# One eviction, one place to turn back and one pair of normalising instructions for the self and cross outputs of a step in a decoder kernel

## What is computed

```python
x = x + self_attention(layernorm(x), Wv, bv, Wo, bo)      # 16 heads of 8
x = x + cross_attention(layernorm(x), ctx, ctx)           # 16 heads of 8, no projection
x = x + experts(layernorm(x), router_w, routing_bias, sw1, sw2, sw3, ew1, ew2, ew3)
# attention: softmax(q k^T / sqrt(8)) v for each head
```

## Times and profile before

| | |
|---|---|
| median of the timed runs | 447.25 us (446.73 to 450.13, 3 runs) |
| span of the profiled execution | 447.9 us |
| PE busy | 420.6 us (94%), 5570 instructions |
| DVE busy | 312.5 us (70%), 767 instructions |
| ACT busy | 300.6 us (67%), 685 instructions |
| POOL busy | 300.5 us (67%), 517 instructions |
| attention steps | from about 10 to about 265 us |
| granted TensorE clock, mean | 0.985 |

### The profile page before, as it was taken

How to read it: one execution, slowest core, us unless ns; L and a number is a source line. 1 busy time by engine, 2 the same in 40 slices (tenths; PEclk the granted TensorE clock), 3 DMA queues, 4 the chain that set the end, 5 groups by cost and what they waited for, 6 DMA issues and landing times. The chain is left out here.

```text
span 447.9 us, 16458 instructions
## 1 busy us (share of the span) xinstructions
PE 420.6 (94%) x5570; PEld 314.2 (70%) x5571; DVE 312.5 (70%) x767; ACT 300.6 (67%) x685; POOL 300.5 (67%) x517
## 2 busy tenths in 40 slices
PE   7889999999999999999999999999999999999990
PEld 4545655555665655555565567899998899999990
DVE  5568999989999999999999854773333444545540
ACT  7858888788888888788888865432222465666650
POOL 8547768677877868687787655278888754444442
PEclk9999999999999999999999999899999999999995
DMA  6243444444444444453433379812222355530010
GB/s 108 37 83 46 77 52 56 69 53 80 57 80 65 70 74 60 88 64 63 46 57 39 32 131 198 268 44 71 77 80 76 85 129 137 137 105 25 27 35 0
DMA packets 181088, 34.51 MB, mean 77 GB/s; under 512 B 147347, under 2 KB 178582, under 8 KB 181024
## 3 DMA queue, kind: packets, MB, share of 16 engines
q1 hardware_dynamic: 170944, 23.63, 33.2%
q0 software_dynamic: 2864, 6.36, 4.1%
q10 hardware_dynamic: 7216, 3.69, 2.9%
HBM read 20.13 MB, written 15.74 MB: 80 GB/s over the span
## 5 line engine op out<-in xcount | busy, mean ns | idle before, releaser
L1162 DVE TENSOR_TENSOR gT<-gT,psum 128x384 f32<-128x384 f32 x66 | 36.6, 554 | 74.2 <-PE psum L744 51.8
L975 ACT ACTIVATE gT<-psum 128x384 f32<-128x384 f32 x70 | 34.1, 487 | 49.4 <-PE psum L744 36.0
L504 POOL DMA_INDIRECT out<-yrow,token x38 | 37.0, 973 | 40.7 <-DVE yrow L1281 26.5
L443 POOL TENSOR_TENSOR k_s<-pT,hmask_sb 128x1024 f32<-128x1024 f32 x32 | 60.9, 1903 | 2.1 <-ACT pT L904 2.0
L758 PE MATMUL psum<-wdn_sb,gT 128*128 (+1 forms) x420 | 59.9, 279 | 2.0 <-DVE yrow L1281 1.0
L409 POOL TENSOR_SCALAR xn_s<-rows_all,mv 128x128 f32<-128x128 f32 x32 | 19.4, 607 | 56.6 <-DVE mv L1060 37.7
L744 PE MATMUL psum<-fhT,wtile 128*128 128x128 f32 x456 | 57.2, 275 | 0.0
L758 PEld LDWEIGHTS psum<-wdn_sb,gT 128*128 128x128 f32 x420 | 52.4, 192 | 5.0 <-issue 3.9
L744 PEld LDWEIGHTS psum<-fhT,wtile 128*128 128x128 f32 x456 | 53.9, 192 | 0.1
L744 PE MATMUL psum<-hT_all,wup_sb 128*128 (+1 forms) x384 | 49.2, 280 | 0.0
L849 ACT COPY prT_x<-psum 128x512 f32<-128x512 f32 x64 | 34.6, 589 | 20.7 <-PE psum L554 20.4
(11 more groups left out here) (150 smaller groups left out, 890.0 us busy)
## 6 DMA issues: line engine op xcount, KB each, us to landing
ring<-sorted_rows SPq DMA_DIRECT2D x30, 130.0 KB
sorted_rows<-nowhere_row SPq DMA_DIRECT2D x38, 65.0 KB, 2.3
wup_sb<-in_wup SPq DMA_DIRECT2D x7, 352.0 KB, 9.6
attention_out<-on_s SPq DMA_DIRECT2D x64, 32.0 KB, 2.9
ring<-in_ctxv SPq DMA_DIRECT2D x64, 32.0 KB, 3.3
orow<-attention_out SPq DMA_DIRECT2D x32, 64.0 KB
sorted_rows<-nowhere_row SPq DMA_DIRECT2D x3, 650.0 KB, 9.1
cross_keys<-in_ctxk ACTq DMA_DIRECT2D x14, 128.0 KB, 3.1
```

Of the source, the lines that this page charges most:

```text
L443: nc.gpsimd.tensor_tensor(k_s[:], pT[:].rearrange("p (b k) -> p b k", b=NB).unsqueeze(2).broadcast_to([P, NB, HG, S]), hmask_sb[:, 0:HG].u ...
L504: pool.indirect_dma_start(out=out, out_offset=bass.IndirectOffsetOnAxis(ap=token[p][:, 0:1], axis=0), in_=yrow[p][:, :], in_offset=None, b ...
L975: nc.scalar.activation(gT[p][:].rearrange("p c q -> p (c q)"), ps_gate[p][:, 0:CH * P], ACT.Silu).then_inc(sem("f_act"), 1)
L1162: nc.vector.tensor_tensor(g, g, ps_up[p][:, 0:CH * P], ALU.mult).then_inc(sem("f_g"), 1)
```

## The change

`oT`, `rden` and `on` become one tile each with a kind index, and so do the two banks' slices (`ps_wT`, `weighed`). `kinds(t)` is the slice of kinds that are weighed in step t: only self for t = 2 to 4, both for t = 5 to 33, only cross for t = 34 to 36. ACT makes one copy of what is live, after both weighings. PE turns back both at the place of the self output, with one semaphore for the two. DVE inverts and normalises both at the place of the self output, the start of the next step. SP (for the write of the self output) and POOL (for the add of the cross output) now wait for the one `on` semaphore. In the hand-written tail of PE the turning back of the cross outputs moves as well: that of unit 29 stands after `turn_rows(2)`, that of unit 30 before `keep_clock(2, bank[4])`, that of unit 31 where it was.

```diff
+        WEIGHED = {"s": LAG["soft_s"], "x": LAG["pv_x"]}
+        def turned_back(t):
+            return t - LAG["soft_s"] + 1
+        def kinds(t):
+            live = [KIND[k] for k in "sx" if 0 <= t - WEIGHED[k] < U]
+            return slice(live[0], live[-1] + 1)
...
-            def turn_back(k, u):
-                pe.wait_ge(sem(f"{k}_oe"), at(u))
-                for g in range(G):
-                    last = nc.tensor.transpose(ps_w[k][:, P * g:P * (g + 1)], oT[k][:, g, :], id_sb[:])
-                last.then_inc(sem(f"{k}_ot"), 1)
+            def turn_back(t):
+                pe.wait_ge(sem("oe"), turned_back(t))
+                for k in "sx"[kinds(t)]:
+                    for g in range(G):
+                        last = nc.tensor.transpose(ps_w[k][:, P * g:P * (g + 1)], oT[:, KIND[k], g, :], id_sb[:])
+                last.then_inc(sem("ot"), 1)
...
-                if live("on_x"):
-                    turn_back("x", u["on_x"])
                 if live("q"):
                     cross_scores(u["q"])
...
                 if live("soft_s"):
-                    turn_back("s", u["soft_s"])
+                    turn_back(t)
...
             query(U - 2)
-            turn_back("x", U - 4)
             route(0, 0)
...
             turn_rows(2)
+            turn_back(U - 3 + WEIGHED["x"])
             turn_output(U - 1)
...
             query(U - 1)
-            turn_back("x", U - 3)
             route(2, 0)
...
-            pe.wait_ge(sem("s_on"), U)
+            turn_back(U - 2 + WEIGHED["x"])
             keep_clock(2, bank[4])
...
-            def evicted(k, u):
-                act.wait_ge(sem(f"{k}_pv"), G * at(u))
-                if u >= 1:
-                    act.wait_ge(sem(f"{k}_ot"), u)
-                nc.scalar.copy(oT[k][:], ps_wT[k]).then_inc(sem(f"{k}_oe"), 1)
+            def evicted(t):
+                for k in "sx"[kinds(t)]:
+                    act.wait_ge(sem(f"{k}_pv"), G * at(t - WEIGHED[k]))
+                if t > LAG["soft_s"]:
+                    act.wait_ge(sem("ot"), turned_back(t - 1))
+                nc.scalar.copy(oT[:, kinds(t), :, :].rearrange("p k g q -> p k (g q)"), ps_wT[:, kinds(t), :]).then_inc(sem("oe"), 1)
...
-                if live("pv_x"):
-                    evicted("x", u["pv_x"])
                 if live("soft_s"):
-                    evicted("s", u["soft_s"])
+                    evicted(t)
...
+            weighed = psum[:, 4:6, G * P:].rearrange("p k (a s c d) -> p k a s c d", a=HP, s=2, c=2)
+            def invert(t):
+                dve.wait_ge(sem("ot"), turned_back(t))
+                nc.vector.reciprocal(rden[:, kinds(t), :, :], weighed[:, kinds(t), :, 1, :, 0]).then_inc(sem("rden"), 1)
+            def normalise(t):
+                dve.wait_ge(sem("rden"), turned_back(t))
...
+                nc.vector.tensor_tensor(on[:, kinds(t), :, :, :], weighed[:, kinds(t), :, 0, :, :],
+                                        rden[:, kinds(t), :, :].unsqueeze(4).broadcast_to([P, len("sx"[kinds(t)]), HP, 2, DK]),
+                                        ALU.mult).then_inc(sem("on"), 1)
...
-                if live("out"):
-                    invert("s", u["out"])
-                    normalise("s", u["out"])
+                if live("out") or live("on_x"):
+                    invert(t - 1)
+                    normalise(t - 1)
...
-                if live("on_x"):
-                    invert("x", u["on_x"])
-                    normalise("x", u["on_x"])
                 if live("q"):
                     maxima("x", u["q"])
```

More of the change, by code:

```diff
@@ L133, in build @@
         prT = {k: sb(f"prT_{k}", [P, G, 4, P]) for k in "sx"}
-        oT = {k: sb(f"oT_{k}", [P, G, P]) for k in "sx"}
-        rden = {k: sb(f"rden_{k}", [P, HP, 2]) for k in "sx"}
-        on = {k: sb(f"on_{k}", [P, HP, 2, DK]) for k in "sx"}
+        KIND = {"s": 0, "x": 1}
+        oT = sb("oT", [P, 2, G, P])
+        rden = sb("rden", [P, 2, HP, 2])
+        on = sb("on", [P, 2, HP, 2, DK])
         orow = [sb(f"orow{i}", [P, D]) for i in range(2)]
@@ L143, in build @@
         ps_o = {"s": bank[4], "x": bank[5]}
-        ps_wT = {k: ps_o[k][:, 0:G * P].rearrange("p (g q) -> p g q", g=G) for k in "sx"}
+        ps_wT = psum[:, 4:6, 0:G * P]
         ps_w = {k: ps_o[k][:, G * P:] for k in "sx"}
@@ L298, in body @@
                 if live("out"):
-                    sp.wait_ge(sem("s_on"), at(u["out"]))
+                    sp.wait_ge(sem("on"), turned_back(t - 1))
                     for b in range(NB):
                         load(sp, o_dram[u["out"], b, :, :, :].rearrange("h q d -> q h d"),
-                             on["s"][S * b:S * (b + 1), :, :, :].rearrange("p a c d -> p (a c) d"), "s_out")
+                             on[S * b:S * (b + 1), KIND["s"], :, :, :].rearrange("p a c d -> p (a c) d"), "s_out")
                 if 0 <= t - 3 < U:
@@ L451, in body @@
                 if live("on_x"):
-                    pool.wait_ge(sem("x_on"), at(u["on_x"]))
+                    pool.wait_ge(sem("on"), turned_back(t - 1))
                     nc.gpsimd.tensor_tensor(x_all[:, u["on_x"], :], x_all[:, u["on_x"], :],
-                                            on["x"][:].rearrange("p a c d -> p (a c d)"), ALU.add).then_inc(sem("x_x"), 1)
+                                            on[:, KIND["x"], :, :, :].rearrange("p a c d -> p (a c d)"), ALU.add).then_inc(sem("x_x"), 1)
                 if live("q"):
@@ L565, in weigh @@
                         pair = NB * (4 * g + i) + b
-                        last = nc.tensor.matmul(ps_wT[k][VW * i:VW * (i + 1), g, S * b:S * (b + 1)],
+                        last = nc.tensor.matmul(ps_wT[VW * i:VW * (i + 1), KIND[k], P * g + S * b:P * g + S * (b + 1)],
                                                 values[:, VW * pair:VW * (pair + 1)],
@@ L722, in _ @@
             turn_rows(5)
-            turn_back("x", U - 1)
+            turn_back(U - 1 + WEIGHED["x"])
             route(4, 1)
@@ L951, in _ @@
             query(U - 2)
-            evicted("x", U - 3)
+            evicted(U - 3 + WEIGHED["x"])
             output(U - 1)
@@ L960, in _ @@
             turned_rows(3)
-            evicted("x", U - 2)
+            evicted(U - 2 + WEIGHED["x"])
             turned_rows(4)
@@ L966, in _ @@
             turned("x", U - 1, 1)
-            evicted("x", U - 1)
+            evicted(U - 1 + WEIGHED["x"])
             for n in range(5, len(HT_BATCHES)):
```

19 lines of the change are left out of this document (5 added, 14 removed).

## The result

The changed kernel takes 461.49 us (median of 4 runs, 460.3 to 462.79); the kernel before, on the same chip, 447.46 us (446.73 to 450.13, 4 runs). The ratio is 1.0306, 95% interval 1.0264 to 1.0349: slower, as forecast (464.5 us, range 458 to 468). The profiled execution has a span of 460.0 us, against 447.9 us; the granted TensorE clock is 0.983.

What follows compares the result with a forecast made beforehand. The self half's closed 7.64 us latency loop was taken as the bound. 29 steps at +0.656 us gave 19.0, less 1.3 for the DRAM row and 0.2 at the ends: +17.5, forecast 464.5 us, range 458 to 468.

Steps and rivals of the forecast that it cites:

- The bound: Self half, eviction to eviction: a closed latency loop of 7.64 us bounds the stage, with VectorE nearly full beside it.
- Eviction, +0.217: ScalarE's copy in the loop: 128x512 at 589 ns replaces 128x256 at 372 ns, +0.217 us a step.
- Transposes back, +0.21: PE, before VectorE's release: four transposes instead of two, 0.69 us instead of 0.48, +0.21 us on both branches.
- Reciprocal +0.095, multiply +0.134: VectorE's merged pair: 32 numbers inverted and 128 more elements multiplied, adding 0.095 and 0.134 us a step.
- Two tied branches: From self transposes to first self exponential, the paths through mean and variance and through self scores both take 3.91 us.
- the link from exponential to `prT_s`: Loop from first self exponential to second `prT_s` copy: 2.16 us, carried over unchanged.
- rival C: No change: leaving PE ahead of the cross scores and VectorE's extra room offset the merging; 447 us, chance 0.05.
- the absorbed waits: PE's waits for the self output row returning through DRAM: 1.3 of 1.9 us disappear in the longer loop.
- the ends, -0.2: Last steps: cross transposes no longer stand between the last query and last cross scores, 0.2 us off.
- A: Rival: VectorE's engine time decides, so each step gets 0.27 us shorter; 439.5 us, chance 0.08.
- B: Rival: only the scores branch ends last or added reading is cheaper, 0.427 us a step or less; 458.2 us, chance 0.16.
- D: Rival: reading two banks is dearer for copy and reciprocal, 5.7 us more in all; 470 us, chance 0.03.

Runs made afterwards that it cites:

- turned_together: Kernel before, with only the cross transposes moved right behind the self transposes, nothing merged; 451.22 us, ratio 1.0014.
- after_copies_apart: Changed kernel, with the eviction as two copies again, cross first, all else merged; 460.15 us, ratio 1.0213.
- query_branch_early: Kernel before, with VectorE's self mean and variance put ahead of those of the two other norms; 452.23 us, ratio 1.0089.
- evict_merged: Kernel before, with only the eviction merged into one 128x512 copy of both kinds; 455.9 us, ratio 1.015.
- after_stats_first_again: Changed kernel, with cross statistics aggregated ahead of the reciprocal and multiply in steps after the last cross query, second run; 464.67 us, ratio 1.0294.
- halves_cross_copy_last: Kernel before, with the self eviction copied in two halves and the cross eviction behind ScalarE's copy of onT; 447.3 us, ratio 0.9976.

## Why the prediction was right, point by point

**The bound.** Right: the closed loop of the self half. In each kernel whose step I read link by link, the typical step moved, within 0.02 us, by what the edit had done to the branch that ends last, in both directions (7.58 to 8.21 us), also where I had forecast the link wrongly.

**Eviction, +0.217.** Measured +0.21 in the link, +0.21 in the step alone, and 8.00 to 8.21 in the changed kernel. The copy over two half banks is no dearer than one over a full bank: 585 ns against 589.

**Transposes back, +0.21.** Right in the branch through mean and variance (0.48 to 0.70). For the branch through the scores it is 0.11, as `turned_together` showed. Since the first one ends last, the sum was not touched by this.

**Reciprocal +0.095, multiply +0.134.** Measured: 0.39 us to the multiply instead of 0.29, 0.34 to the add instead of 0.21: +0.23, as forecast. `after_copies_apart` confirms both in the step: 0.21 for the transposes, 0.23 for the pair and -0.10 for the link below make 0.34, and 8.00 - 7.64 is 0.36.

**Two tied branches.** They tie in the kernel before, within 0.05 us. That both take 3.91 us to the same exponential did not show it yet; the experiments do. `turned_together` and `query_branch_early` delay the maxima by 0.11 and 0.17 and not the query, and the step grows by 0.10 and 0.16. The other branch lengthens the step by itself in some steps of the kernel before, in which the aggregate comes 0.35 us late (below): with the maxima at 2.12 the exponential could start at 4.10 there, and it starts at 4.26. After, the maxima start at 158.50, 1.41 us behind the scores instead of 1.23: they wait on VectorE for the self aggregate, not for PE. I had that branch fall behind by 0.23 and forgot that it crosses the other one on VectorE. It made no difference.

**First mis-sized term: the link from exponential to `prT_s`.** I carried 2.16 us over; it is 2.06 in every step. The two self exponentials take 1.14 us together instead of 1.23, but that alone doesn't do it: in `evict_merged` they take 1.14 too, and the link is still 2.16. What differs is when PE starts to transpose their result. First `evict_merged`, where the cross transposes (at 154.90) still stand ahead of the cross scores (L557), then the changed kernel (its exponentials start at 160.65):

```profile
155.27 0.21 PEld L557 LDWEIGHTS psum<-ring,qT 64*64 64x64 f32 x8 [0.17 <-issue]
155.30 1.14 ACT L854 ACTIVATE pr_s<-pr_s 128x512 f32<-128x512 f32 x2
156.29 0.85 PEld L566 LDWEIGHTS psum<-id_sb,pr_s 128*128 128x128 f32 x8 [0.81 <-ACT pr_s L854]
```

```profile
160.24 0.21 PEld L557 LDWEIGHTS psum<-ring,qT 64*64 64x64 f32 x8 [0.20 <-issue]
...
161.32 0.94 PEld L566 LDWEIGHTS psum<-id_sb,pr_s 128*128 128x128 f32 x8 [0.87 <-ACT pr_s L851]
```

In `evict_merged`, as in the kernel before, PE gets to them 1.02 us behind the start of the cross scores, 0.99 us behind the first exponential. With the cross transposes out of the way the cross scores start 0.41 us ahead of the exponential instead of 0.03, and PE begins at 0.67. The long steps of `turned_together` have 0.67, 1.14 and 2.06 as well; its short steps have 0.82, 1.23 and 2.16. So the 0.10 us needs both: the cross transposes gone from there, and the second exponential ready in time. My sentence that they go "from a stretch with slack" was wrong: this is the mechanism of rival C, and it pays a seventh of the price back. Over 26 steps it is 2.2 us that I had too many (+0.57 a step instead of +0.656).

**Second: the absorbed waits.** I took 1.3 us off for the row through DRAM. The right reckoning is the excess of all steps over the typical one: before 202.34 - 26 x 7.64 = 3.7 us, after 214.35 - 26 x 8.21 = 0.9. So 2.8 us of lateness disappeared. 1.5 of them are not the row's. In six steps of the kernel before an aggregate on VectorE comes 0.23 to 0.37 us late, though the profile names nothing that it waits for; its DVE rows in one of them:

```profile
126.26 0.28 DVE L1120 TENSOR_TENSOR rows_all<-psum,rows_all 128x128 f32<-128x128 f32 x1
...
127.11 0.18 DVE L1060 BATCH_NORM_AGGREGATE mv<-st_p 128x2 f32<-128x6 f32 x1 [0.23 <-issue]
127.31 0.18 DVE L1060 BATCH_NORM_AGGREGATE mv<-st_s 128x2 f32<-128x6 f32 x1
```

From the add to the self aggregate are 1.05 us there instead of 0.69; query and exponential come 0.35 us later, and the step is 7.99 us instead of 7.64. The six add up to 1.9 us. The changed kernel has two such steps (0.35 and 0.10). `turned_together` and `evict_merged`, with the pairs on VectorE as before, have six; `after_copies_apart`, with the merged pair, has two: so it goes with the change on VectorE, and what it is stays open. The remaining 1.3 us is what I had forecast for the row through DRAM.

**Third: the ends, -0.2.** Measured +1.7, of which 1.3 lie between the last multiply and GpSimd's add (1.81 us instead of 0.51): VectorE's order in the last steps, as `after_stats_first_again` shows. I looked there for what PE loses and gains and not at what stands behind the pair on VectorE.

**The base.** I put the profiled execution 0.65 us above the median, by comparing its span with the times of runs. A run's time is its span plus 1.8 us (461.82 and 460.0; 467.03 and 465.2), so the profiled execution of the kernel before took 449.7, 2.2 above the median of 447.46. The forecast isn't touched by this, since what it amounts to is the change added to the median, 447.25 + 17.5. (The upper bound of the reciprocal comes to 0.40, not 0.39, by its own working; that moves nothing either.)

Together: 17.5 forecast, less 2.2 for the link and 1.5 for the late aggregates, less 0.4 in the first three steps (1.54 measured, 3 x 0.656 = 2.0 forecast), plus 1.9 for the ends, is 15.3; the profile has 12.1, or 15.2 with the 3.1 us of its short expert stage put back. Measured by the medians are 14.0 us against 17.2 forecast. The four loop prices were right to 0.02 us each. That the sum came within 3 us is in part luck, as the miss at the ends took back half of the others.

**The rivals.** A fell with `evict_merged`: less work for ScalarE, slower. For the multiply and the reciprocal it fell with `after_copies_apart`. B's time (458.2) is almost as near to the measurement (3.3 us) as the forecast (3.0), but its mechanism isn't there: the pair is paid in full. C, as no change, fell with the result, but part of its mechanism is real: leaving the place ahead of the cross scores gives 0.10 us a step in the changed kernel, though nothing in the short steps of `turned_together`. D's dearer reading of two banks isn't in the rows.

**The rule of one large tile.** The prices follow it: the merged copy takes 585 ns where two take 744. The Trainium skill, "VectorE: DVE Perf Modes", section "The TRN2 errata — SBUF-src ops pay a fixed extra latency per instruction", gives ScalarE, from PSUM, 172 cycles and one per column at 1.2 GHz. An estimate from that page's figures is 570 ns for 512 columns and 357 for 256; the rows have 585 and 372. The rule counts engine time, and here engine time wasn't the bound.

## What to carry to other kernels

Merging two small instructions saves the fixed part of one, which is a gain only where their engine is the bound. Where one of the two is ready early and the other lies in a latency loop, the merged one starts with the later and takes longer than the later alone, so the loop pays in every step for a half that had been free; look for that first. When an instruction moves, read what stands behind it on its engine, at the place that it leaves as well as at the new one, and in the last steps too: the cross transposes were worth 0.10 us a step at their old place, and work in the gap of a chain costs nothing, while beside the gap it costs up to all of its length.

## What the runs showed of the hardware

- A `RECIPROCAL` of 128x32 from PSUM takes 358 ns, of 128x16 258 in the kernel before's loop (0.26 in the earlier trace rows) and 246 in the changed kernel's tail: 6 to 7 ns an element, where the multiply has 1.03 (424 ns for 128x256 and 292 for 128x128).
- A ScalarE copy or a VectorE multiply over two banks of PSUM costs no more than its elements would in one: 585 ns for 2 x 256 columns against 589 for 512.
- The same aggregate on VectorE started 0.23 to 0.37 us late in six of 26 steps of the kernel before, with no releaser named, and 0.35 and 0.10 us late in two of the changed kernel's. The cause stays open.
- In the profile of `halves_cross_copy_last` the granted clock was 0.52 from 27 to 32 us, near the 1.2 GHz level, with PE busy for all 5 us, behind 5 us in which PE was busy for 3.49 (clock 0.80). It was 1.00 from 27 to 32 us in the kernel before and in two kernels with the same wait. What set it off stays open.
